# The square root of a piece's variance ahead of the first Silu, its normalisation ahead of the output weights, and the block decay kept by a maximum

## The chip, the cores and the metric

The kernel is written for one Trainium2 chip and runs on one of its cores. A core has five engines that work side by side: TensorE (PE), VectorE (DVE), ScalarE (ACT), GpSimd (POOL), and SyncE (SP), which here only issues DMAs. Each runs its own list of instructions in order and waits on semaphores. The metric is the time of one execution on the device, in microseconds; lower is better.

## The reference

`x` is (2, 1024, 512) in fp32. Two blocks follow each other, each with a layernorm ahead, a layernorm behind and a residual:

```
x = x + layernorm(attention(layernorm(x)))
x = x + layernorm(ffn(layernorm(x)))

attention(h):                        # 32 heads of 128
    q, k, v = silu(h @ qkv_w.T)      # per head
    # linear attention with a decay per head, in blocks; kv is the state
    scores = (q k^T) * diag_decay
    out    = scores v + (q * q_decay) kv
    kv     = kv * block_decay + (k * k_decay)^T v
    out    = norm_w * out * rsqrt(mean(out^2) + eps)
    return (sigmoid(h @ gate_w.T) * out) @ out_w.T
ffn(h):                              # 512 -> 1792 -> 512, integer weights with scales
    return (silu(h @ gate.T) * (h @ up.T)) @ down.T
```

The layernorm needs a mean and a variance of each token, and the square root of the variance plus 1e-5.

## The kernel before

**Tiling.** The tokens are cut into 16 tiles of 128, four segments of 512, two batches of 1024. The heads go in 16 pairs. One *step* `w` is a head pair of one batch; there are 32 steps (0 to 31), the 16 pairs for batch 0 and then the 16 for batch 1. Step 0 is written out apart. In step `w` the kernel projects K, Q, V and the gate G of that step, and finishes the attention and the output projection of the step before (`a = w - 1`). A projection is not a plain product: a 2x2 block scheme with seven products (numbered 1 to 7) and sums of their results (`keep_s1` on ACT, `keep_s2`, `keep_s3`, `finish_22`, `finish_12`, `finish_21` on DVE) takes the place of eight. Each fp32 operand is split in a high and a low part, so that each product is three matmuls for each of two row blocks.

**Order.** Every engine has a function `window(w, ...)` that writes out by hand the order of its instructions within a step; there is no planner. The engines keep together by counting semaphores alone. Hardware loops (`Fori`) repeat it. SP's `window` gives the order of the DMAs: weights, the K blocks written to DRAM (`k_write`, behind two transposes `turn_k` on DVE, line 1510) and read back turned (`k_read`), and the same for V (`v_write`, `v_read`, `turn_v` on line 1518).

**Pieces.** The input of batch 1 must be layernormed, transposed and put through the scheme's sums before step 16 needs it. That is spread over steps 1 to 8 as eight *pieces* of 2 x 128 tokens, the argument `part`. For a piece DVE takes statistics at the end of the step before (`statistics_of_piece`, the variance plus epsilon on line 1627, behind the two V transposes), ACT takes the root (`piece_root`, line 1012, both columns at once), DVE makes the reciprocal and the shift (`scales_of_piece`, lines 1633 and 1635), ACT normalises two tiles (`normalise_piece`, line 1018), PE transposes them (`turn_piece`, line 2189, four transposes ahead of product 7 of Q), ACT copies them out (`keep_piece`), DVE forms sums (`mix_piece`), ACT and POOL split and ACT stores them. From step 17 on, `finish` does the same for tiles of batch 0 ahead of the FFN; I call steps 18 to 25 tile steps. Steps 9 to 15 have no piece but a check of the FFN's integers on DVE (`look_at_block`, whose maximum is line 1570).

**ACT's tables.** Silu, Sigmoid and Sqrt each need another table of ACT. A load (`ACT_TABLE_LOAD`) stands in the trace ahead of an instruction whose table isn't the one that is loaded, and runs before that instruction's wait is over; none stands ahead of Copy, Square and Identity.

**The lines the prediction follows.** ACT, step `w`: `keep_s1(w, KK)` (Copy of K), Silu of K's block 11, `keep_s1(w, QQ)` (Copy of Q, line 910), then the root, `split_out_hi` (line 894, waits for the scaled output weights), `split_hi_s` (line 888), Silu of K's block 22 (line 926), `normalise_piece`, `square(a, 0, 0)` (line 940), `gated_hi`, `split_hi_a`, two Silus, `square(a, 0, 1)`. DVE: `gate(a, s, h)` (line 1555) waits for that Square, since it reads the same attention result; behind `gate(a, 0, 1)` come `turn_k(w, 1, 0)`, `turn_k(w, 1, 1)`, `update_state`, `keep_s3(w, QQ)` (line 1473), `turn_k(w, 0, 0)`, which waits until the K blocks are written (`k_out`), and `finish_22(w, QQ)` (line 1481). PE waits for `keep_s3` ahead of product 3 and for `finish_22` ahead of product 4:

```
                if i == 3:
                    pe.wait_ge(s3_done, n)
                if i == 4:
                    pe.wait_ge(c22_done, n)
```

`keep_b` (line 1534) saves the two block decays of a step out of `table`, 128 x 2 values, so that the table can be loaded anew while `update_state` of that step still needs them. It runs in each of the 32 steps.

Of the kernel before, what the change touches and what calls it, by code (L numbers as in the profile page):

```python
# [25 lines left out]
TAB_D, TAB_Q, TAB_K, TAB_B = 0, 2 * P, 4 * P, 4 * P + 2  # L26
# [50 lines left out]
def products_until(w, kind, i):  # L77

    if isinstance(w, int) and w == 0:
        return FIRST_ORDER.index((kind, i)) + 1  # L80
    return PRODUCTS * w - FEWER + ORDER.index((kind, i)) + 1
# [7 lines left out]
def sums_until(w, kind):  # L89

    return 4 * w + kind - 1
# [34 lines left out]
def sandwich_kernel(nc, x, w_attn, w_out, norm_w, tables, w_ints, ffn_scales, down_s, out):  # L126
    ctx = ExitStack()
    with ctx:
        def sem(name):
            return ctx.enter_context(nc.semaphore(name))  # L130

        def sb(name, shape, dt=F32, scope=ctx):
            return scope.enter_context(nc.sbuf_tensor(name, shape, dt))
# [24 lines left out]
        b_prev = sb("b_prev", [P, 2])  # L158
# [35 lines left out]
        table_in, b_kept = sem("table_in"), sem("b_kept")  # L194
# [70 lines left out]
        table = sb("table", [P, TAB], scope=two)  # L265
# [563 lines left out]
        def _(act):  # L829
# [83 lines left out]
            def activate(w, kind, out_block):  # L913

                n = sums_until(w, kind)
                dst = projected(kind, out_block)
                if out_block == OUT11:
                    act.wait_ge(proj_done, products_until(w, kind, 2))
                    src = blocks_view(kind, chain(kind, 0)[:, :])
                else:  # L920
                    act.wait_ge({OUT22: c22_done, OUT12: c12_done, OUT21: c21_done}[out_block], n)
                    src = dst
                if kind == GG:
                    act.activation(dst, src, ACT.Sigmoid).then_inc(gate_done, 1)
                else:
                    act.activation(dst, src, ACT.Silu).then_inc(silu_done, 1)  # L926
# [50 lines left out]
            def tile_root(i):  # L977

                act.wait_ge(tile_step, 5 * i + 3)
                act.activation(tile_stdev[:, 0:1], tile_var[:, 0:1], ACT.Sqrt).then_inc(tile_sd_ready, 1)  # L980
# [28 lines left out]
            def piece_root(j):  # L1009

                act.wait_ge(piece_step, 7 * j + 5)
                act.activation(tile_stdev[:, :], tile_var[:, :], ACT.Sqrt).then_inc(piece_sd_ready, 1)

            def normalise_piece(j):

                act.wait_ge(piece_step, 7 * j + 7)
                for s in range(HALVES):
                    act.activation(tiles[:, s], tiles[:, s], ACT.Identity, bias=tile_shift[:, s:s + 1],  # L1018
                                   scale=tile_rstd[:, s:s + 1]).then_inc(piece_normed, 1)
# [37 lines left out]
            def window(w, next_weights=True, checks=None, first_done=False, finish=None, begin=None,  # L1057
                       part=None, next_part=None, into_ffn=False):
# [6 lines left out]
                    square_root(norm_a[1])  # L1065
                if finish is not None:
                    tile_root(finish)
                activate(w, KK, OUT11)
                keep_s1(w, QQ)
                if part is not None:  # L1070
                    piece_root(part)
                split_out_hi(a)
                if finish is not None:
                    normalise_tile(finish)
                split_hi_s(w, VV)
                activate(w, KK, OUT22)
                if part is not None:
                    normalise_piece(part)
                square(a, 0, 0)
                gated_hi(a, 0, 0)  # L1080
                split_hi_a(w, VV)
# [299 lines left out]
        def _(dve):  # L1381
# [74 lines left out]
            def scale_out_weights(a):  # L1456
                dve.wait_ge(ow_in, 16 * (a + 1))
                dve.wait_ge(norm_in, 16 * (a + 1))
                for h in range(2):
                    dve.tensor_scalar(ow[:, h], ow[:, h], nw[:, h:h + 1], None,  # L1460
                                      ALU.mult).then_inc(ow_scaled, 1)
# [8 lines left out]
            def keep_s3(w, kind):  # L1470

                dve.wait_ge(proj_done, products_until(w, kind, 5))
                dve.tensor_tensor(projected(kind, OUT22), blocks_view(kind, chain(kind, 1)[:, :]),
                                  projected(kind, OUT12), ALU.add).then_inc(s3_done, 1)
# [56 lines left out]

            def keep_b(n):

                dve.tensor_copy(b_prev[:, :], table[:, TAB_B:TAB_B + 2]).then_inc(b_kept, 1)

            def update_state(a, s, h):
                dve.wait_ge(contrib_done, att_until(a, s, h))
# [92 lines left out]
            def scales_of_piece(j):  # L1630

                dve.wait_ge(piece_sd_ready, j + 1)
                dve.reciprocal(tile_rstd[:, :], tile_stdev[:, :]).then_inc(piece_step, 1)
                dve.wait_ge(piece_step, 7 * j + 6)
                dve.scalar_tensor_tensor(tile_shift[:, :], tile_meanvar[:, :, 0], -1.0, tile_rstd[:, :],
                                         ALU.mult, ALU.mult).then_inc(piece_step, 1)
# [11 lines left out]
            def window(w, first=False, checks=None, rms_of=None, ends_first=False, finish=None, begin=None,  # L1648
                       part=None, next_part=False, v_second=v_tok):
# [11 lines left out]
                if finish is not None:  # L1661
                    scales_of(finish)
                keep_s3(w, KK)
                scale_out_weights(a)
                finish_22(w, KK)
                finish_12(w, KK)
                if part is not None:
                    scales_of_piece(part)
                gate(a, 0, 0)
                finish_21(w, KK)  # L1670
                keep_s2(w, QQ)
# [768 lines left out]
```

## Time and profile before

| | us |
|---|---|
| median of 3 runs | 2396.22 |
| lowest and highest | 2396.11, 2396.77 |
| the profiled execution: first to last instruction (its span) | 2391.0 |
| busy: PE, POOL, DVE, ACT | 2350.5, 1679.5, 1379.5, 1207.6 |
| granted clock of PE, mean | 0.997 of full speed |

For the profiled execution the page gives the span alone; the time of an execution also holds what lies ahead of its first and behind its last instruction, so the span stands 5.2 us below the median of the runs. Busy times of the engines overlap. The ends of matmuls are modelled: an engine row of PE may run over the start of the next one, and the idle time in front of a PE row is then shown too short. The starts are measured.

### The profile page before, as it was taken

To read this page: it belongs to the slowest core of one execution; us is meant where nothing else is said; L and a number is where in the kernel's file an instruction comes from. 1 tells how busy PE (TensorE), PEld (TensorE's weight loads), DVE (VectorE), ACT (ScalarE), POOL (GpSimd) and SP (SyncE) were. 2 spreads that over 40 slices of the span, in tenths; PEclk is the share of its full clock that TensorE was granted. 3 is DMA by queue.
4 is the path that set the end of the run, shared out by engine and by line. 5 is a ranking of instruction groups with operands and counts; after the bars stand their busy time and mean duration, and the time that the engine had idled before them with its cause. 6 is when DMAs were issued, how large, how long until landed. Compare 5 with 4: busy or idle time off the path is not lost.

```text
span 2391.0 us, 38298 instructions
## 1 busy us (share of the span) xinstructions
PE 2350.5 (98%) x12276; PEld 2002.1 (84%) x12276; DVE 1379.5 (58%) x2475; ACT 1207.6 (51%) x1748; POOL 1679.5 (70%) x1322
## 2 busy tenths in 40 slices
PE   7999999999999999999999999999999999999997
PEld 6788888888888888878888888888888888888886
DVE  5555555555666666656555555555555555555655
ACT  6555555555444444435554555444444444466563
POOL 4667777777777777766777777777777776574675
PEclk9999999999999999999999999999999999999999
DMA  4334444444444444564443343444333333511212
GB/s 136 127 127 143 134 126 126 141 143 143 143 131 130 137 145 135 160 203 146 141 137 131 121 132 129 140 141 128 114 106 111 113 119 116 211 62 71 80 62 98
DMA packets 165954, 307.16 MB, mean 128 GB/s; under 512 B 22384, under 2 KB 102256, under 8 KB 163184
## 3 DMA queue, kind: packets, MB, share of 16 engines
q1 hardware_dynamic: 138992, 269.93, 34.7%
q10 hardware_dynamic: 26880, 36.18, 4.6%
q8 instruction: 46, 0.75, 0.1%
q14 instruction: 36, 0.29, 0.0%
HBM read 219.02 MB, written 87.03 MB: 128 GB/s over the span
## 4 chain that ended last, share of the span: by engine, by line
PE 89%; ACT 3%; DMA 3%; issue 2%; DVE 2%; POOL 0%; SPq 0%; DVEq 0%; ACTq 0%; POOLq 0%
PE proj L2012 54%; PE yp L2012 18%; PE sc L2059 5%; PE sc L2082 4%; PE sc L2085 4%; PE sc L2072 4%; DMA k_blocks<-pd 2%; DVE pd L1510 1%; ACT piece L1018 0%; ACT k L926 0%; ACT L926 0%; ACT sq L940 0%; DMA y<-x 0%; DVE g L1555 0%; ACT w_even L888 0%
## 5 line engine op out<-in xcount | busy, mean ns | idle before, releaser
L2012 PE MATMUL proj<-xb,w_odd 128*128 128x512 f32 x2694 | 704.9, 399 | 7.3 <-DVE q L1481 2.7
L2012 PE MATMUL proj<-xb,w_even 128*128 128x512 f32 x2694 | 678.4, 395 | 8.0 <-DVE xb L1425 3.3
L2012 PEld LDWEIGHTS proj<-xb,w_even 128*128 128x128 f32 x2694 | 496.9, 189 | 110.1 <-issue 5.9
L2012 PEld LDWEIGHTS proj<-xb,w_odd 128*128 128x128 f32 x2694 | 489.6, 189 | 106.2 <-DVE q L1481 6.9
L610 POOL TENSOR_TENSOR qd<-q,table 128x512 f32<-128x512 f32 x128 | 164.0, 1293 | 193.7 <-ACT q L926 193.7
L1555 DVE TENSOR_TENSOR g<-sc,g 128x512 f32<-128x512 f32 x128 | 88.4, 691 | 296.8 <-ACT sq L940 296.8
L601 POOL TENSOR_TENSOR ow_lo<-v_tok,ow_hi 128x1024 fp32r<-128x1024 f32 x32 | 76.7, 2397 | 224.0 <-ACT ow_hi L894 224.0
L1562 DVE TENSOR_TENSOR y<-yp,y 128x512 f32<-128x512 f32 x240 | 164.3, 685 | 120.5 <-PE yp L2012 119.2
L2012 PE MATMUL proj<-x_t,f_hi 128*128 128x512 f32 x896 | 212.6, 389 | 0.0
L2012 PE MATMUL yp<-ow_hi,g_hi 128*128 128x512 f32 x512 | 202.3, 395 | 0.3 <-issue 0.3
L595 POOL TENSOR_TENSOR w_odd<-ws,w_odd 128x1024 fp32r<-128x1024 f32 x63 | 151.3, 2401 | 69.5 <-ACT w_odd L888 69.5
L2012 PE MATMUL yp<-ow_hi,g_lo 128*128 128x512 f32 x512 | 199.5, 390 | 0.0
L2012 PE MATMUL yp<-ow_lo,g_hi 128*128 128x512 f32 x512 | 199.3, 389 | 0.0
L2012 PEld LDWEIGHTS proj<-x_t,f_hi 128*128 128x128 f32 x896 | 168.0, 188 | 34.9
L2082 PE MATMUL sc<-pd,v 128*128 128x128 f32 x1024 | 186.9, 274 | 0.0
L2085 PE MATMUL sc<-qd,state 128*128 128x128 f32 x896 | 173.2, 275 | 0.0
L626 POOL TENSOR_TENSOR g_lo<-g,g_hi 128x512 fp32r<-128x512 f32 x128 | 163.5, 1298 | 8.9 <-ACT g_hi L945 8.9
L2082 PEld LDWEIGHTS sc<-pd,v 128*128 128x128 f32 x1024 | 159.5, 191 | 10.0
L622 POOL TENSOR_TENSOR sumsq<-sumsq,sq 128x512 f32<-128x512 f32 x124 | 160.8, 1297 | 4.7
L731 POOL TENSOR_TENSOR h_lo<-hid,h_hi 128x512 fp32r<-128x512 f32 x56 | 73.3, 1310 | 112.1 <-ACT h_hi L1278 112.0
L933 ACT ACTIVATE kd<-k_tok,table 128x512 f32<-128x512 f32 x128 | 85.5, 716 | 131.4 <-DMA k_tok<-k_blocks 131.4
L595 POOL TENSOR_TENSOR w_even<-ws,w_even 128x1024 fp32r<-128x1024 f32 x63 | 151.9, 2411 | 0.0
(194 smaller groups left out, 4405.6 us busy)
## 6 DMA issues: line engine op xcount, KB each, us to landing
raw<-w_attn SPq DMA_DIRECT2D x128, 512.0 KB, 3.8
k_blocks<-pd SPq DMA_DIRECT2D x64, 512.0 KB, 3.6
k_tok<-k_blocks SPq DMA_DIRECT2D x256, 128.0 KB, 2.8
v_blocks<-vf SPq DMA_DIRECT2D x64, 512.0 KB, 2.7
v_tok<-v_blocks SPq DMA_DIRECT2D x248, 128.0 KB, 2.8
v_tok<-w_out SPq DMA_DIRECT2D x32, 512.0 KB, 4.5
fraw<-w_ints SPq DMA_DIRECT2D x13, 1024.0 KB, 4.8
piece<-w_ints ACTq DMA_DIRECT2D x21, 512.0 KB, 4.4
```

Source lines behind the costliest of these rows:

```text
L595: pool.tensor_tensor(w_lo[slot][:, S_1:S_4 + 1], ws[:, :, :, :], w_hi[slot][:, S_1:S_4 + 1].bitcast(F32), ALU.subtract).then_inc(wlo_s_don ...
L610: pool.tensor_tensor(qd[:, s, h].rearrange("p (c n) -> p c n", c=CH), q[:, h, half(s)].rearrange("p (c n) -> p c n", c=CH), decay.unsqueez ...
L622: pool.tensor_tensor(total, total, sq[:, h], ALU.add).then_inc(ss_done, 1)
L626: pool.tensor_tensor(g_lo[:, h], g[:, h, half(s)], g_hi[:, h].bitcast(F32), ALU.subtract).then_inc(glo_done, 1)
L933: act.activation(kd[:, s, h].rearrange("p c (i d) -> p i c d", i=QUADS), k_tok[:, :, h], ACT.Copy, scale=table[:, TAB_K + h:TAB_K + h + 1] ...
L1555: dve.tensor_tensor(at, sc[h][:, :], at, ALU.mult).then_inc(gated_done, 1)
L1562: dve.tensor_tensor(y[:, t], yp[t % 2][:, :], y[:, t], ALU.add).then_inc(yacc_done, 1)
L2012: last = pe.matmul(psum, s, m, start=start and n == 0, stop=n == len(terms) - 1, skip_group_check=more)
L2059: last = pe.matmul(sc[h][:, chunk(c)], k[:, h, tok], q[:, h, tok], start=True, stop=True)
L2072: last = pe.matmul(sc[h][:, chunk(c)], kd[:, s, h, c], v[:, s, c, h], start=True, stop=True)
L2082: last = pe.matmul(sc[h][:, chunk(c)], v[:, s, c, h], pd[:, s, h, c], start=True, stop=not inter)
L2085: last = pe.matmul(sc[h][:, chunk(c)], state[:, h, (c - 1) % CH], qd[:, s, h, chunk(c)], start=False, stop=True)
```

## The change

In steps 1 to 8 ACT takes the root of the piece's variance ahead of Silu of K's block 11, not behind the Copy of Q, and normalises the piece straight behind the Copy of Q, not behind Silu of K's block 22. DVE makes the piece's reciprocal and shift straight behind `keep_s3(w, KK)`, ahead of the scaling of the output weights, not behind `finish_12(w, KK)`. In all steps `keep_b` copies the two block decays by a maximum of them with themselves (`tensor_tensor` with `max`), where it was `tensor_copy`; the values are the same. No instruction is added or taken away in the code, no DMA and no semaphore changes.

```diff
--- before.py
+++ after.py
@@ -1065,17 +1065,17 @@
                     square_root(norm_a[1])
                 if finish is not None:
                     tile_root(finish)
+                if part is not None:
+                    piece_root(part)
                 activate(w, KK, OUT11)
                 keep_s1(w, QQ)
                 if part is not None:
-                    piece_root(part)
+                    normalise_piece(part)
                 split_out_hi(a)
                 if finish is not None:
                     normalise_tile(finish)
                 split_hi_s(w, VV)
                 activate(w, KK, OUT22)
-                if part is not None:
-                    normalise_piece(part)
                 square(a, 0, 0)
                 gated_hi(a, 0, 0)
                 split_hi_a(w, VV)
@@ -1531,7 +1531,8 @@
 
             def keep_b(n):
 
-                dve.tensor_copy(b_prev[:, :], table[:, TAB_B:TAB_B + 2]).then_inc(b_kept, 1)
+                kept = table[:, TAB_B:TAB_B + 2]
+                dve.tensor_tensor(b_prev[:, :], kept, kept, ALU.max).then_inc(b_kept, 1)
 
             def update_state(a, s, h):
                 dve.wait_ge(contrib_done, att_until(a, s, h))
@@ -1661,11 +1662,11 @@
                 if finish is not None:
                     scales_of(finish)
                 keep_s3(w, KK)
+                if part is not None:
+                    scales_of_piece(part)
                 scale_out_weights(a)
                 finish_22(w, KK)
                 finish_12(w, KK)
-                if part is not None:
-                    scales_of_piece(part)
                 gate(a, 0, 0)
                 finish_21(w, KK)
                 keep_s2(w, QQ)
```

## Rows read from the trace of the kernel before

Idle time ahead of an instruction stands in brackets, with what ended it. In the rows of stretches the columns are: from and to, length, then for PE, PEld, DVE, ACT and POOL the busy time with the number of instructions, PE's granted clock, DMA share and GB/s.

**Rows 1.** The page, part 1: busy time, share of the span, instructions.
```profile
PE 2350.5 (98%) x12276; PEld 2002.1 (84%) x12276; DVE 1379.5 (58%) x2475; ACT 1207.6 (51%) x1748; POOL 1679.5 (70%) x1322
```

**Rows 2.** Stretches: steps 1 to 8, step 8, step 9, one tile step.
```profile
74.13:589.90 515.77, 510.35 (x2716) 434.05 (x2715) 297.02 (x574) 274.19 (x409) 381.39 (x306) 1.00 0.42 132
525.25:589.90 64.65, 64.03 (x342) 54.41 (x341) 37.05 (x73) 34.22 (x52) 48.14 (x40) 1.00 0.42 131
589.90:652.56 62.66, 62.66 (x338) 53.97 (x337) 41.03 (x67) 29.20 (x43) 46.90 (x39) 1.00 0.43 140
1161.41:1224.54 63.13, 63.13 (x342) 54.31 (x341) 36.11 (x67) 31.63 (x48) 45.80 (x38) 1.00 0.40 133
```

**Rows 3.** Waits of PE, steps 1 to 8: us, times, longest.
```profile
PE proj L2012 <- DVE q L1481: 1.7, 5, 0.4
PE yp L2189 <- ACT piece L1018: 1.6, 6, 0.3
PE proj L2012 <- DVE q L1473: 0.7, 4, 0.2
PE proj L2012 <- DVE k L1473: 0.5, 2, 0.3
```

**Rows 4.** ACT in order of time, step 3: start, us.
```profile
202.86 0.60 ACT L910 ACTIVATE k<-proj 128x512 f32<-128x512 f32 x1 [0.96 <-PE proj L2012]
...
207.71 0.60 ACT L926 ACTIVATE k<-proj 128x512 f32<-128x512 f32 x1 [2.95 <-PE proj L2012]
211.33 0.60 ACT L910 ACTIVATE q<-proj 128x512 f32<-128x512 f32 x1 [3.03 <-PE proj L2012]
211.95 1.28 ACT L1012 ACT_TABLE_LOAD   x1
...
213.36 1.04 ACT L894 ACTIVATE ow_hi<-v_tok 128x1024 fp32r<-128x1024 f32 x1
...
215.36 1.28 ACT L926 ACT_TABLE_LOAD   x1
...
217.19 1.50 ACT L1018 ACTIVATE piece<-piece,tile_shift,tile_rstd 128x512 f32<-128x512 f32 x2
218.60 0.58 ACT L940 ACTIVATE sq<-sc 128x512 f32<-128x512 f32 x1
...
222.34 0.58 ACT L940 ACTIVATE sq<-sc 128x512 f32<-128x512 f32 x1
```

**Rows 5.** PE in order of time, step 3.
```profile
218.16 0.39 PE L2085 MATMUL sc<-qd,state 128*128 128x128 f32 x2
218.83 0.65 PE L2189 MATMUL yp<-ident,piece 128*128 128x128 f32 x4 [0.28 <-ACT piece L1018]
...
226.50 1.65 PE L2012 MATMUL proj<-xb,w_odd 128*128 128x512 f32 x6 [0.18 <-DVE q L1473]
...
229.86 1.66 PE L2012 MATMUL proj<-xb,w_odd 128*128 128x512 f32 x6 [0.34 <-DVE q L1481]
```

**Rows 6.** DVE in order of time, step 3.
```profile
206.05 0.47 DVE L1627 TENSOR_SCALAR tile_var<-tile_meanvar 128x2 f32<-128x2 f32 x1
...
211.06 0.88 DVE L1460 TENSOR_SCALAR v_tok<-v_tok,nw 128x512 f32<-128x512 f32 x2 [0.40 <-DMA nw<-norm_w]
...
223.56 1.29 DVE L1510 STREAM_TRANSPOSE pd<-k 128x512 f32<-128x512 f32 x2
...
228.52 0.71 DVE L1510 STREAM_TRANSPOSE pd<-k 128x512 f32<-128x512 f32 x1 [2.07 <-DMA k_blocks<-pd]
```

**Rows 7.** Single lines of DVE: ns min/median/max, first and last start in us.
```profile
L1534 DVE COPY b_prev<-table x32: 157/160/1536, 72.0 to 2036.1; 128x2 f32<-128x2 f32 x32
...
L1570 DVE TENSOR_TENSOR maxima<-maxima x21: 552/1021/1900, 609.3 to 1016.2; 128x1 f32<-128x1 f32 x21
...
L1635 DVE SCALAR_TENSOR_TENSOR tile_shift<-tile_meanvar,tile_rstd x8: 160/161/2292, 85.5 to 536.8; 128x2 f32<-128x2 f32 x8
```

**Rows 8.** DVE in order of time, step 8.
```profile
529.91 0.23 DVE L1627 TENSOR_SCALAR tile_var<-tile_meanvar 128x2 f32<-128x2 f32 x1
```

## The prediction

> **What bounds the kernel now.** I read the page first. TensorE (PE) is busy for 98% of the span [rows 1]. So an edit on ScalarE (ACT) or VectorE (DVE) can pay only where PE stands still, and the question is where, if anywhere, steps 1 to 8 hold it.
>
> The view of the stretches answers that [rows 2]. I cut it at the start of each step's first Copy of the K projection. Step 9 has no piece: 62.66 us, PE busy throughout. A tile step has the same four extra PE transposes as a piece step: 63.13 us, PE busy throughout. So 0.47 us is the fair price of four transposes. Steps 1 to 8 together take 515.77 us, where eight tile steps would take 505.04. The excess is 10.73 us, 1.34 us a step, and nothing else in the kernel runs at this discount. That is the most this change could give if it mended all of it. The idle time that the same row shows, 515.77 - 510.35 = 5.4 us, is smaller, because the modelled ends of matmuls run over part of each hole. I therefore use lengths, and the waits only for shares.
>
> The waits of PE in these eight steps name four releasers [rows 3]: the normalisation of the piece (1.6 us), DVE's line 1481 for Q (1.7), line 1473 for Q (0.7) and line 1473 for K (0.5). The first three are 4.0 of 4.5.
>
> Step 3 shows where they sit [rows 5]. The transposes of the piece start at 218.83, though PE's stream before them (pairs of 128-column matmuls from 218.16, a pair every 0.22) would be through at 218.39: a hole of 0.44. The row's own idle time is 0.28, so the modelled end hides 0.16. Product 3 of Q starts at 226.50 after 0.18 idle, so a hole of about 0.34; product 4 of Q at 229.86 after 0.34 idle, so about 0.50.
>
> ACT's order explains all three [rows 4]. After the Copy of Q at 211.33 it loads the square root's table (1.28), takes the root (0.13 to the next start), splits the output weights and the V sums, loads Silu's table again (1.28), runs a Silu, the two normalisations (1.50), and only then Square of head 0 (218.60) and of head 1 (222.34). DVE waits for that second Square: the K transposes start at 223.56, their write to DRAM has to land, the next transpose starts at 228.52 after a wait on that DMA, and behind it stands the finish of Q's block 22 that releases PE at 229.86 [rows 6]. Line 1473 for Q stands behind the same K transposes. So one lateness of ACT makes three holes. Meanwhile ACT idles 2.95 us ahead of its first Silu [rows 4].
>
> **The change, part by part.**
>
> *The root ahead of the first Silu.* It needs the variance, whose DVE instruction starts at 206.05 and takes 0.47, so 206.52 [rows 6]. The root's table is loaded before that: the load behind the Copy of K is through when the idle time begins, at 204.76. Then the root (to 206.7), the load of Silu's table (1.28 and a gap of some hundredths), and the first Silu starts near 208.1, not 207.71: 0.4 us later. The tile steps run just this order, and PE is busy throughout in them [rows 2]. Behind this Silu on ACT stands the Copy of Q at 211.33, with 3.03 us of idle before it. Cost: nothing. If the variance came after 209.2 (211.33 less 0.2 for the root, 1.3 and 0.6 for the Silu) the cover would be gone. That is 6.3 us into step 3, which starts at 202.86 [rows 4]. In step 8 the variance is done 4.9 us into the step (529.91 + 0.23 against 525.25), where step 3 has it after 3.7 [rows 2, 8]; 1.4 us are still left.
>
> *What leaves the stretch behind the Copy of Q.* Root's table and root 1.41 (from 211.95 to the next start, 213.36), Silu's table 1.28: about 2.7 us [rows 4]. The sequence has three table loads a step where it had four, and the one that is left over falls into ACT's idle time.
>
> *The normalisation ahead of the output weights.* It takes 1.41 us start to start (217.19 to 218.60), in the place where the load and the root took 1.41. The split of the output weights therefore still starts at about 213.4, GpSimd (POOL) and PE behind it see no change, and everything after Silu of block 22 comes 2.7 us sooner: Square of head 0 at 215.9, of head 1 at 219.6. PE has given attention of head 1 by 218.4, so that is not what holds it.
>
> *The scales on DVE.* Two small instructions, about 0.16 each [rows 7], move from behind the finishes of K to 210.66, where DVE is now free until 211.06 [rows 6]. They need the root, ready at 206.7. Behind them waits the scaling of the output weights, at 211.06 after 0.40 idle for a DMA: 0.36 with a gap fits in 0.40. Without that cover ACT would have the scaled weights 0.4 later (at 212.3), and it takes them at 213.4. Cost nothing.
>
> *The block decay by a maximum.* One DVE instruction of 128x2 in each of 32 steps, no DMA, no new wait. The copy takes 160 ns in the middle and 1536 at most [rows 7]. No maximum of this shape is in the trace. From below: a small DVE instruction on two SBUF inputs that nothing hinders, the shift at line 1635, is 160 at the least and 161 in the middle [rows 7]. From above: the 128x1 maximum of the width checks takes 552 to 1900, middle 1021 [rows 7]. So tiny an instruction can't be at work that long: something holds it. The copy is held too, up to 1.5 us, but in few steps, and what holds the one at this place in the step should hold the other. So I take the copy's time, a cost of 0; the upper end is the rival below. The Trainium skill (SBUF — State Buffer, section "Who interferes with whom") says that a DVE instruction with two SBUF inputs contends with a GpSimd instruction that reads SBUF, as does a copy in a two-port mode. By that rule both forms are exposed alike, the change of form buys nothing, and the rows agree as far as they go.
>
> *Where the stall goes.* Hole 1: the piece is normalised at about 213.3 and PE comes at 218.39: gone, 5 us of slack. Hole 2 and 3: K transposes at 220.9, the one behind the DMA at 225.8 with the same landing time, Q's block 22 ready for PE at 229.86 - 2.7 = 227.2. PE, now early by all three holes (0.44 + 0.34 + 0.50), wants it at 228.58. So 1.4 us of slack: gone as well. Line 1473 for Q has more. What is late next is that DMA: were it 1.4 us longer, hole 3 would come back.
>
> **Sum.** By shares, 10.73 x 4.0/4.5 = 9.5 us. Not mended directly is line 1473 for K, whose 0.5 us come from a late V transpose at the start of two steps. Since ACT and POOL get about 1 us further ahead of PE, one of these two (step 8) may close too; I add 0.2. Gain 9.7 us: the span 2391.0 becomes 2381.3. The runs' median 2396.22 lies 5.2 us above the profiled span, and I keep this distance: **2386.5 us**, 0.4% faster.
>
> **The rivals.**
>
> *A part of the holes stays.* The write of the K blocks, issued sooner beside a weight load, takes over 1.4 us longer in some steps, or DVE reaches line 1473 late for another reason. Then PE keeps hole 3, or 2 and 3. For it speaks that this DMA is in the path; against it that the landing now is followed by slack. Keeping hole 3 in all steps (1.7 of 4.5, of 10.73) costs 4.1: gain 5.6, 2390.6.
>
> *The releasers named are not the real ones.* PE's holes in 2 and 3 might be the DMA's alone, whatever ACT does, and the first hole moves to the next wait. Against it stand steps 9 and on, without root or normalisation and with no hole [rows 2]. Then at most the transposes' hole goes (1.6 of 4.5, of 10.73: gain 3.8, 2392.4), at least nothing (2396.2); both are within 0.2%.
>
> *Slower: the maximum is held by POOL everywhere.* If it waits for a whole POOL operation (the longest of the checks' maxima, 1.9 us) in each of 31 steps, the V transposes, the V read behind them and line 1473 for K are late in the next step. Step 8 shows the price: the variance, which stands behind these transposes, starts 4.66 us into the step against 3.19 in step 3, and these 1.47 gave a hole at K's product 3 of about 0.44 (its longest wait, 0.3, and the 0.16) [rows 3, 6, 8]. So a hold counts from about 1.03 us. At 1.9 in 31 steps: 31 x 0.87 = 27 lost, 9.7 gained, 2413. It decides from 1.03 + 9.7/31 = 1.34 us in every step. Against it: the copy takes 160 ns in the middle, so nothing holds it in most steps.
>
> *The table loads cost more than their rows.* The Trainium skill (ScalarE: Activation LUTs, section "What ACT_TABLE_LOAD costs") puts a drain of about 1.4 us on top of the load; here the next instruction starts 1.30 us after the load's start, so the trace doesn't show it. By the page ACT would gain still more, and the time would be the same, since PE is the limit.
>
> **How the numbers follow.** All three holes go (gain 8.4 to 10.9: from a step or two that keeps one, to all of the excess): 0.77. A part stays: 0.12. Not the real releasers: 0.07 (within 0.2%). Slower by the maximum: 0.04. The runs differ by 0.7 us and a measurement can tell 0.2%, 4.8 us, from no change. Likeliest 2386.5; its own range 2385.0 to 2388.0. The range of 8 in 10 reaches a little into the partial case: 2384.6 to 2389.8. Faster by over 0.2%: 0.77 + 0.12 = 0.89; within 0.2%: 0.07; slower 0.04.
>
> **What the profile after would show.** Steps 2 to 7 are 63.1 us long, where 515.77/8 is 64.5, and PE is busy in all of the stretch. ACT has the root at about 206.7 in step 3's place, three table loads a step, the normalisation straight behind the Copy of Q. PE waits neither for line 1018 nor for line 1481. The copy's successor takes 0.16 us in most steps and up to 1.5 in some. Wrong would be: steps that stay at 64; a wait of PE on the K write's chain at the old place; a DVE instruction of over 1 us at the decay in most steps, with longer steps from 9 on.

## The result and the profile after

The changed kernel takes 2383.6 us, median of 5 executions (2382.43 to 2384.59), against 2396.11 for the kernel before, also 5 (the three behind 2396.22 and two more; 2393.24 to 2396.77). The ratio is 0.9948, with a 95% interval of 0.9937 to 0.9958. The change gains 12.5 us, where 9.7 were forecast. The time lies 1.0 us below the foot of the range that I gave. In the experiments further down, one of the 11 executions of before_again took 11691 us at a granted clock of 0.19, and its ratio leaves that one out.

The profiled execution of the changed kernel took 2383.29 us for a span of 2381.4. The page, part 1, of the kernel after:

```profile
PE 2345.7 (98%) x12276; PEld 2002.7 (84%) x12276; DVE 1381.2 (58%) x2475; ACT 1196.6 (50%) x1740; POOL 1678.2 (70%) x1322
```

ACT has eight instructions fewer than in [rows 1], 1740 for 1748: one table load less in each piece step. DVE and POOL are as they were.

Stretches of the kernel after: steps 1 to 8, then step 3, step 5 and step 9 (columns as in [rows 2]).

```profile
73.23:579.10 505.87, 504.38 (x2715) 433.97 (x2715) 297.94 (x574) 263.42 (x402) 381.47 (x306) 1.00 0.42 135
199.03:261.96 62.93, 62.93 (x341) 54.27 (x340) 37.54 (x73) 32.83 (x50) 47.16 (x39) 1.00 0.43 137
325.17:389.56 64.39, 64.39 (x349) 55.51 (x348) 36.18 (x72) 32.81 (x50) 47.05 (x39) 1.00 0.39 126
579.10:641.76 62.66, 62.66 (x338) 53.95 (x337) 41.44 (x67) 29.29 (x43) 46.26 (x39) 1.00 0.42 136
```

The first row stands against 515.77 in [rows 2]: 9.90 us less. Step 3 is 62.93 long; before it was 64.48. Step 9, without a piece, has its old length to the hundredth (62.66). The one piece step that still stands out is step 5 with 64.39. The waits of PE in steps 1 to 8 show the same (us, times, longest):

```profile
PE proj L2013 <- DVE k L1467: 0.8, 1, 0.8
PE proj L2013 <- DVE k L1473: 0.6, 2, 0.3
```

Of [rows 3] only line 1473 for K is left. The normalisation and both waits of Q are gone, in all eight steps. Line 1467 for K is new, once (in step 6, behind the long step 5; see "What stays open").

ACT in step 3, whose first Copy starts at 199.03, 3.83 us sooner than in [rows 4]. To compare two rows, take each from its own step's start.

```profile
199.03 0.60 ACT L910 ACTIVATE k<-proj 128x512 f32<-128x512 f32 x1 [1.37 <-PE proj L2013]
199.65 1.28 ACT L1012 ACT_TABLE_LOAD   x1
202.32 0.20 ACT L1012 ACTIVATE tile_stdev<-tile_var 128x2 f32<-128x2 f32 x1 [1.39 <-DVE tile_var L1628]
202.54 1.28 ACT L926 ACT_TABLE_LOAD   x1
203.88 0.60 ACT L926 ACTIVATE k<-proj 128x512 f32<-128x512 f32 x1
207.51 0.60 ACT L910 ACTIVATE q<-proj 128x512 f32<-128x512 f32 x1 [3.03 <-PE proj L2013]
208.00 1.51 ACT L1018 ACTIVATE piece<-piece,tile_shift,tile_rstd 128x512 f32<-128x512 f32 x2
...
211.83 0.58 ACT L940 ACTIVATE sq<-sc 128x512 f32<-128x512 f32 x1
...
215.57 0.57 ACT L940 ACTIVATE sq<-sc 128x512 f32<-128x512 f32 x1
```

The root starts 3.29 us into the step and the first Silu at 4.85, which was 4.85 before too (207.71 - 202.86): the load and the root are covered. The Square of head 1 starts 16.54 us into the step, where it was 19.48: 2.94 sooner.

DVE in step 3:

```profile
206.95 0.16 DVE L1636 SCALAR_TENSOR_TENSOR tile_shift<-tile_meanvar,tile_rstd 128x2 f32<-128x2 f32 x1
...
216.78 1.29 DVE L1510 STREAM_TRANSPOSE pd<-k 128x512 f32<-128x512 f32 x2
...
223.01 0.71 DVE L1510 STREAM_TRANSPOSE pd<-k 128x512 f32<-128x512 f32 x1 [2.32 <-DMA k_blocks<-pd]
223.65 0.65 DVE L1481 TENSOR_TENSOR q<-proj,q 128x512 f32<-128x512 f32 x1
```

The product of PE that [rows 5] had wait for line 1481 starts at 224.62, with no idle time ahead of it.

The K transposes start 17.75 us into the step, 2.95 sooner than in [rows 6] (20.70). But the transpose behind the DMA starts at 23.98, against 25.66: only 1.68 sooner. So 1.27 us of the gain went between the two, and SP's queue shows where. First before, then after (start, duration of the issue):

```profile
223.48 0.33 SPq L378 DMA_DIRECT2D raw<-w_attn  x1
224.88 0.33 SPq L395 DMA_DIRECT2D k_blocks<-pd  x1
228.51 1.76 SPq L402 DMA_DIRECT2D k_tok<-k_blocks  x4
```

```profile
217.25 0.33 SPq L378 DMA_DIRECT2D raw<-w_attn  x1
218.11 0.33 SPq L395 DMA_DIRECT2D k_blocks<-pd  x1
223.00 1.75 SPq L402 DMA_DIRECT2D k_tok<-k_blocks  x4
```

The reads of line 402 wait until the K write of line 395 has landed. Before, the write was issued 1.40 us behind the weight load and 3.63 us later it had landed. After, it stands 0.86 behind the load and takes 4.89. The other steps are alike: in the eight piece steps the write is 1.40 to 1.54 behind and lands in 3.35 to 3.70 before, 0.77 to 0.90 behind and in 4.38 to 4.89 after. DVE has `finish_22(Q)` at 223.65 + 0.65 = 224.30 and PE comes at 224.62: 0.3 us of slack, where I had counted 1.4.

### The profile page after: what moved, and what is told of

Read it like the earlier page. It is cut to its first block, busy times and chain, and to the rows that moved or that the text cites. A ratio compares the mean times of both kernels' runs of the same rounds, so it can differ in the third digit from the quotient of the medians.

```text
span 2381.4 us, 38290 instructions
## 1 busy us (share of the span) xinstructions
PE 2345.7 (98%) x12276; PEld 2002.7 (84%) x12276; DVE 1381.2 (58%) x2475; ACT 1196.6 (50%) x1740; POOL 1678.2 (70%) x1322
## 4 chain that ended last, share of the span: by engine, by line
PE 79%; issue 1%; DMA 1%; DVE 1%; POOL 1%; ACT 1%; SPq 0%; DVEq 0%; ACTq 0%; POOLq 0%
PE proj L2013 48%; PE yp L2013 16%; PE sc L2083 4%; PE sc L2060 4%; PE sc L2086 3%; PE sc L2073 3%; DMA k_blocks<-pd 0%; DMA v_tok<-v_blocks 0%; DMA k_tok<-k_blocks 0%; DMA v_blocks<-vf 0%; POOL w_odd L588 0%; PE yp L2181 0%; PE sc L2121 0%; ACT sq L940 0%; DVE pd L1510 0%
## 5 line engine op out<-in xcount | busy, mean ns | idle before, releaser
L2083 PEld LDWEIGHTS sc<-pd,v 128*128 128x128 f32 x1024 | 160.0, 191 | 10.1
```

Source lines behind the costliest of these rows:

```text
L2083: last = pe.matmul(sc[h][:, chunk(c)], v[:, s, c, h], pd[:, s, h, c], start=True, stop=not inter)
```

## The experiments

Twelve runs were made, in three groups, each with executions of the kernel before on the same chip (medians 2397.55, 2398.07 and 2397.54 in the groups). I give the ratio to these. "Steps 1 to 8" is the length of that stretch in the one profiled execution. All theories are about these steps. The rest of the span is 1873.5 to 1880.3 us long in the fourteen traces, whatever the order in the piece steps (before 1875.2, before_again 1878.2, after 1875.5, order_only 1877.9).

**The kernel before, once more** (before_again). No edit.

> The kernel before, unchanged, to see how its executions spread and how span and time stand to each other. Theory: the time is the span plus about 1.9 us, as in the five executions of the changed kernel (1.9 to 2.1), and the profiled execution of before (span 2391.0) was a short one; most executions then have a span of about 2394.2, and the 3 us lie in places that one trace doesn't show. Rival: before really has 5.2 us around its span; then its spans are near 2391.0 in every execution. Time 2396.1 by both.

2396.42 us, ratio 0.9998 (0.9988 to 1.0007). Its stretches: steps 1 to 8, then step 5; and PE's waits in steps 1 to 8.

```profile
73.73:591.95 518.22, 510.88 (x2718) 434.57 (x2717) 303.15 (x574) 274.02 (x410) 381.27 (x306) 1.00 0.41 131
...
331.81:398.34 66.53, 65.88 (x355) 56.04 (x353) 38.91 (x72) 34.12 (x52) 47.84 (x39) 1.00 0.39 123
```

```profile
PE proj L2012 <- DVE q L1481: 2.5, 8, 0.5
PE yp L2189 <- ACT piece L1018: 1.9, 7, 0.3
PE proj L2012 <- DVE k L1467: 1.3, 1, 1.3
PE proj L2012 <- DVE q L1473: 0.8, 5, 0.2
```

The same program is 2.45 us longer in these steps than in the trace that I had. Step 5 alone makes 2.1 of it (66.53 against 64.40): at its end DVE was late, since a V read landed late, and ACT's next Copy of K came late behind it; PE then waited 1.34 us for line 1467, 5.14 us into step 6. The other steps differ from the trace before by less than 0.2 us each. The profiled execution took 2398.45 us for a span of 2396.4, and in every execution whose span is listed, of every kernel, the time is 1.86 to 2.15 us above the span. The 21 executions of the kernel before in this group have spans of 2391.9 to 2399.7 with a median of 2395.5. So the execution behind [rows 1 to 8], with 2391.0, was a short one.

**The order alone, and the maximum alone** (order_only, max_only).

```diff
# order_only
+                if part is not None:
+                    piece_root(part)
                 activate(w, KK, OUT11)
                 keep_s1(w, QQ)
                 if part is not None:
-                    piece_root(part)
+                    normalise_piece(part)
                 split_out_hi(a)
...
                 activate(w, KK, OUT22)
-                if part is not None:
-                    normalise_piece(part)
...
                 keep_s3(w, KK)
+                if part is not None:
+                    scales_of_piece(part)
                 scale_out_weights(a)
                 finish_22(w, KK)
                 finish_12(w, KK)
-                if part is not None:
-                    scales_of_piece(part)
```

```diff
# max_only
-                dve.tensor_copy(b_prev[:, :], table[:, TAB_B:TAB_B + 2]).then_inc(b_kept, 1)
+                kept = table[:, TAB_B:TAB_B + 2]
+                dve.tensor_tensor(b_prev[:, :], kept, kept, ALU.max).then_inc(b_kept, 1)
```

> The moves on ScalarE and VectorE alone, the block decay still a copy. Theory: all of the gain is the moves', 2383.6 us, within 0.7. Rival: the maximum makes the 2.8 us by which the prediction fell short, and this kernel takes 2386.4.

> The maximum alone, in the old order. Theory: no change, 2396.1 us. Rival 1: the maximum is worth 2.8 us, 2393.3. Rival 2: the maximum costs, by up to 1.3 us beside GpSimd in 8 steps, and the moves gained more than they showed: 2397 to 2398.

The order alone: 2383.72 us, 0.9943 (0.993 to 0.9957), steps 1 to 8 504.24. PE waits once in them, 0.3 us for line 1473 of K in step 1, and steps 2 to 8 are 62.93 to 63.21 long.

```profile
74.25:578.49 504.24, 503.95 (x2718) 434.26 (x2717) 299.45 (x574) 263.07 (x401) 381.43 (x306) 1.00 0.43 135
```

The maximum alone: 2396.0 us, 0.9996 (0.9987 to 1.0005), steps 1 to 8 517.73. The whole gain is the order's.

The decay's instruction by itself: the copy in before_again, then the maximum in max_only (ns min/median/max).

```profile
L1534 DVE COPY b_prev<-table x32: 157/164/3118, 72.1 to 2041.3; 128x2 f32<-128x2 f32 x32
```

```profile
L1535 DVE TENSOR_TENSOR b_prev<-table x32: 139/156/3117, 72.6 to 2039.2; 128x2 f32<-128x2 f32 x32
```

Both forms are held, and up to the same 3.12 us.

**The root early, the normalisation where it was** (root_only): order_only without the move of `normalise_piece`.

> Root ahead of the first Silu and scales early, normalisation at its old place behind Silu of block 22, block decay a copy. Theory: what counts is the 2.7 us of table loads and root that leave ScalarE's stretch ahead of the two Squares; the normalisation stands ahead of them either way, so 2383.6 us like the moves together. Rival: the place of the normalisation counts by itself (the piece ready 5 us ahead of TensorE's transposes rather than 2.4): 2386 to 2388.

2383.76 us, 0.9944 (0.9931 to 0.9958), steps 1 to 8 504.16. The move of the normalisation adds nothing that can be measured to the moves of the root and the scales. It even costs slack. SP in step 3 of root_only, which starts at 200.37:

```profile
218.19 0.33 SPq L378 DMA_DIRECT2D raw<-w_attn  x1
219.57 0.33 SPq L395 DMA_DIRECT2D k_blocks<-pd  x1
223.38 1.75 SPq L402 DMA_DIRECT2D k_tok<-k_blocks  x4
```

Here the write stands 1.38 us behind the weight load and lands in 3.81, and `finish_22(Q)` is through 1.3 us ahead of PE (224.67 against 225.95), where the kernel after has 0.3. The rows say what the normalisation has to do with it. The load is issued when POOL's line 588 has ended (218.02 here, 218.14 in order_only, with the load at 218.30). That line waits for ACT here. In order_only the output weights' split comes later behind the normalisation, POOL starts on its sums 1.3 us later in the step and runs through without a gap, and the load goes out 0.4 us later in the step (18.21 against 17.82), while the write goes out 0.1 us sooner.

**The scales left behind the finishes of K** (scales_late): order_only without DVE's part.

```diff
# scales_late: order_only, but with
                 keep_s3(w, KK)
-                if part is not None:
-                    scales_of_piece(part)
                 scale_out_weights(a)
                 finish_22(w, KK)
                 finish_12(w, KK)
+                if part is not None:
+                    scales_of_piece(part)
```

> ScalarE as in the change, but VectorE makes the piece's scales at the old place, behind the finishes of K (to 213.84 in step 3 of before); block decay a copy. The normalisation then holds ScalarE for 1.9 us behind the Copy of Q. Theory: what counts is when the two Squares come; here they come 0.9 us earlier than before where the change gives 2.9. Hole 1 goes, hole 2 all but goes, of hole 3 about 0.4 us a step stays: steps of 63.5 us, 2387 us, against 2383.7 with the scales early. Rival: the scales' place does not matter, 2383.7.

2397.26 us, 0.9999 (0.9991 to 1.0008), steps 1 to 8 517.71. No gain at all, where I had expected 2387. Its waits of PE in steps 1 to 8, then PE and SP in step 3, which starts at 204.06:

```profile
PE proj L2012 <- DVE q L1481: 10.1, 8, 1.5
```

```profile
231.21 1.65 PE L2012 MATMUL proj<-xb,w_odd 128*128 128x512 f32 x6 [1.40 <-DVE q L1481]
```

```profile
224.23 0.33 SPq L378 DMA_DIRECT2D raw<-w_attn  x1
225.09 0.33 SPq L395 DMA_DIRECT2D k_blocks<-pd  x1
229.86 1.75 SPq L402 DMA_DIRECT2D k_tok<-k_blocks  x4
```

The waits for the normalisation and, but for 0.2 us in step 1, for line 1473 of Q are mended, as in the kernel after. Yet product 4 of Q starts 27.15 us into the step, and in the kernel before it started at 27.00 (229.86 - 202.86, [rows 4, 5]). ACT is 1 us sooner here (DVE has the K transposes at 223.77, 19.71 into the step, against 20.70), but the write is again 0.86 behind the weight load and lands in 4.77 us instead of 3.63, which takes that 1 us back. So the start of product 4 is set by the chain through the K write alone; in all eight steps PE waits for line 1481 there, 0.92 to 1.54 us. Holes 1 and 2 ahead of it only shorten hole 3: closing them gives nothing as long as that chain ends last.

**The pieces' root left out** (no_table): the old order, with the piece's square root replaced by a Copy, so that no table is loaded for it. The pieces are then scaled wrongly.

```diff
-                act.activation(tile_stdev[:, :], tile_var[:, :], ACT.Sqrt).then_inc(piece_sd_ready, 1)
+                act.activation(tile_stdev[:, :], tile_var[:, :], ACT.Copy).then_inc(piece_sd_ready, 1)
```

> The old order and the old copy, but the piece's root is replaced by a Copy: the square root is left out for the pieces, and with it two table loads a step. Theory: the two loads (2.6 us ahead of the Squares) are the cost, not the order in itself; 2383.7 us and steps of 63.1. Rival: the order matters by more than its loads (the normalisation ahead of the transposes): 2386 to 2388, with a wait of TensorE for the normalisation left.

2387.28 us, 0.996 (0.9947 to 0.9973), steps 1 to 8 507.68. With the old order kept and only the two table loads out of ACT's stretch, three quarters of the gain are there (9.6 us by the ratio, where the kernel after has 12.5). The time is not the 2383.7 of my theory but lies where the rival had it. The rival's sign, a wait of PE for the normalisation, is absent all the same: steps 2, 3, 4, 7 and 8 have the lengths of the kernel after to 0.01 us, with the root, the scales and the normalisation all at their old places. What is missing in the trace against the kernel after, 1.8 us, is in step 1 (64.07 against 62.75, with 0.3 us of wait left for line 1481) and in steps 5 and 6. What makes the rest of the 2.9 us between the two gains no trace shows. ACT gains less here than the loads give, since DVE's shift, at its old place but sooner, is held for about 2 us in every step and the normalisation waits for it (1.05 us in step 3):

```profile
L1635 DVE SCALAR_TENSOR_TENSOR tile_shift<-tile_meanvar,tile_rstd x8: 1966/2032/2299, 85.7 to 529.4; 128x2 f32<-128x2 f32 x8
```

So the K transposes start 19.14 us into step 3, 1.56 sooner than before, but the write keeps its 1.39 behind the load and lands in 3.54, and hole 3 is closed. It is the loads that held ACT, not the place of the root as such.

**The normalisation early, the root late** (norm_early_root_late): one move more in the old order.

```diff
                 if part is not None:
                     piece_root(part)
+                    normalise_piece(part)
...
                 activate(w, KK, OUT22)
-                if part is not None:
-                    normalise_piece(part)
```

> Root at its old place behind the Copy of Q, the normalisation straight behind it, VectorE in the old order, four table loads a step, block decay a copy. TensorE finds the piece ready. Theory: the wait for the normalisation goes, but the Squares come 0.4 us later than before, so holes 2 and 3 grow by what hole 1 gives back and 0.4 more: steps of 64.9 us, 2399.5 us. Rival: the three holes are separate, and the first one's share is gained: 2392.4.

2404.91 us, 1.0032 (1.0021 to 1.0043), steps 1 to 8 523.77: 7.7 us slower than the kernel before by the ratio, where I had expected 2399.5. In its step 3 (start 204.81) ACT waits for the scales, and Square of head 1 comes 0.72 us later in the step than before, not 0.4:

```profile
216.01 1.52 ACT L1018 ACTIVATE piece<-piece,tile_shift,tile_rstd 128x512 f32<-128x512 f32 x2 [0.61 <-DVE tile_shift L1634]
```

PE then waits most for line 1472 of that kernel (1473 of the kernel before), 6.4 us in eight waits. So the early normalisation does harm unless the root and the scales are early too, and with them it gives nothing (root_only). The root's move alone, with the scales and the normalisation at their old places, wasn't run. No_table, which has both at their old places and no loads, gives every step but 1, 5 and 6 its full gain; this suggests that the root's move alone would do most of it, but doesn't show it.

**The decay's instruction behind the V transposes** (decay_late): the kernel after, with `keep_b(w)` moved behind `turn_v(w, 0, 0)` and `turn_v(w, 0, 1)` in every step that begins no tile, steps 1 to 8 among them.

> The changed kernel, with the maximum behind the two V transposes of head 0 and 1 rather than ahead of them. In the changed kernel it is held by up to 1.4 us in steps 1 to 8, beside GpSimd. Theory: this hold has cover (the V transposes have 1 us to spare in most steps), so within 0.2% of it, at most 0.5 us faster: 2383.2. Rival: the hold still costs some tenths in each of the eight steps and is behind the hole at step 5: 2381 to 2382.

2385.45 us, 0.9952 (0.9939 to 0.9965), steps 1 to 8 505.38. No gain over the kernel after. My rival of 2381 to 2382 isn't borne out; that the instruction is held at that place costs nothing that can be measured.

**The K write ahead of the weight load** in SP's queue, in the kernel of scales_late, the kernel before and the kernel after (scales_late_kfirst, before_kfirst, after_kfirst), with the kernel after once more beside them (after_again).

```diff
-                if next_weights:
-                    weights(w + 1, KK, ...)
-                k_write(w, 1)
+                k_write(w, 1)
+                if next_weights:
+                    weights(w + 1, KK, ...)
                 k_read(w, 1)
```

> As the kernel with the late scales, which gained nothing though two of the three holes had gone, but SyncE issues the write of the second segment's K blocks ahead of the next step's K weights, not behind them. In the kernel with the late scales the write came 0.86 us behind that weight load and took 4.7 us to land, where in before it came 1.4 behind it and took 3.6. Theory: the write shares the DMA engines with the weight load, and that took back what the earlier Squares gave; without the load ahead it lands in about 3 us and hole 3 (1.3 to 1.6 us a step) goes: 2384 to 2387 us. Rival: the landing has nothing to do with the load, hole 3 stays: 2396 to 2397.

> The kernel before with only that exchange on SyncE. Theory: hole 3 (0.2 to 0.7 us a step) goes, since it is set by the landing, and holes 1 and 2 stay; gain 8 x 0.5 = 4 us, 2392 to 2393, and a smaller spread of the executions. Rival: no change, 2396.4.

> The changed kernel with that exchange on SyncE. TensorE finds Q's block 22 ready 0.3 us ahead in the changed kernel; with the write landing in 3 us and not 4.9 it would be 2 us ahead. Theory: nothing to gain any more in most steps, 2383.6, at most 1 us less. Rival: the later K weights delay the sums of GpSimd and so later steps: 2384 to 2386.

> The changed kernel once more, on the chip on which the kernel before has its time of 2396 to 2398, for a second trace. Theory: 2383.6, span 1.9 to 2.1 below the time, steps 1 to 8 together 504 to 506 us against 517 to 518 in the traces of the old order; the late V read at step 5 is in some traces and not in others. Rival: the gain of 12.5 was the chip's, and here it is 9.7.

| kernel | us | ratio | steps 1 to 8 |
|---|---|---|---|
| scales_late_kfirst | 2384.04 | 0.9944 (0.9931 to 0.9958) | 506.54 |
| before_kfirst | 2389.95 | 0.9971 (0.996 to 0.9982) | 511.47 |
| after_kfirst | 2383.91 | 0.9938 (0.9924 to 0.9951) | 504.19 |
| after_again | 2383.1 | 0.9937 (0.9923 to 0.9951) | 506.37 |

SP of scales_late_kfirst in step 3 (start 200.23):

```profile
221.37 0.33 SPq L395 DMA_DIRECT2D k_blocks<-pd  x1
221.99 0.33 SPq L378 DMA_DIRECT2D raw<-w_attn  x1
224.29 1.76 SPq L402 DMA_DIRECT2D k_tok<-k_blocks  x4
```

The write is issued 21.14 us into the step, no sooner than in scales_late (21.03), and lands in 2.92 us instead of 4.77. The 10.1 us of waits for line 1481 are gone (what is left of PE's waits in the eight steps is 0.9), and the kernel gains what the kernel after gains. So what took scales_late's gain was the write's landing behind the weight load.

PE's waits of before_kfirst in steps 1 to 8:

```profile
PE yp L2189 <- ACT piece L1018: 2.2, 8, 0.3
PE proj L2012 <- DVE k L1467: 1.3, 1, 1.3
PE proj L2012 <- DVE q L1473: 1.1, 7, 0.2
```

Here hole 3 is gone and holes 1 and 2 are left. Steps 2 to 8 are 63.84 to 64.12 long, each 0.85 to 0.93 more than the same step of order_only, where the prediction had read 0.44 + 0.34 = 0.78 for the two. This exchange alone gets 0.9971, about half of the change's gain. On the kernel after it adds nothing that can be measured: the 0.3 us of slack is enough there.

## Why the prediction was right in its mechanism and short in its size

**The bound and its place**, that PE stands still only in steps 1 to 8 and at three holes in each: right. All three are gone in all eight steps, and in step 3 the root is through 3.49 us into the step (202.32 + 0.20 - 199.03), where the working had 3.84 (206.7 - 202.86), since the variance is ready sooner too. So the rivals by which the releasers aren't the real ones, or a part of the holes stays, are out for this kernel.

**The root ahead of the first Silu**, covered by ACT's idle time: right (first Silu 4.85 us into the step before and after; the 0.4 us by which the working had it later didn't come). **What leaves the stretch**, 2.7 us of loads and root: right, the Square of head 1 comes 2.94 sooner; no_table shows that it is the loads. The 0.24 beyond 2.7 are gaps that went with them: where no load stands between, ACT's next instruction starts some 0.1 us before the end of the one ahead (the normalisation at 208.00, the Copy of Q until 208.11).

**The scales on DVE, "Cost nothing"**: true of their price, but with the normalisation early they carry the result: scales_late gains nothing. I had called that move free where it was needed. With the normalisation at its old place the late scales don't stop the gain (no_table), so the need is one that the early normalisation makes.

**The block decay by a maximum, a cost of 0**: right, by max_only, though the argument's top, "up to 1.5 us, but in few steps", was low: the copy is held in most of steps 1 to 8, and for 3.12 us in one of before_again. The rival that went by this hold is out: both forms are held alike.

**"With the same landing time"**: wrong. The write lands in 4.9 us instead of 3.6, since DVE comes 2.9 us sooner and the weight load ahead of it in the queue only 2.4 (18.22 into the step for 20.62). Of "1.4 us of slack" 0.3 was left. The sentence that the gain would fail "were the DMA 1.4 longer" was the right one: it got 1.27 longer in step 3. The kernel after escapes by 0.3; scales_late, where ACT gains only 1 us, doesn't. In root_only the landing is nearly the old one (3.81) and the slack 1.3, as counted: what broke the premise is the early normalisation, by way of POOL and the weight load.

**The sum is the step that failed: "By shares, 10.73 x 4.0/4.5 = 9.5", with its 0.2 a "gain 9.7".** It gave 9.7 where 12.5 were measured. The mechanism was right, the term was mis-sized, and three things are in it.

First its form. Holes on one path don't add up as shares. The K write's chain lets product 4 start 27.00 us into the step, and PE without holes is there at 25.59 (224.62 - 199.03): this difference of 1.41 is nearly all of the 1.55 by which step 3 became shorter. Closing the two holes ahead of it would have given nothing, as scales_late shows, and the rival "keeping hole 3 costs 4.1" should have read: costs nearly all. Since all three close, all of the excess of 10.73 goes and not 9.7: 1.0 us more.

Second the length without holes. I took eight tile steps, 505.04. In order_only and root_only the eight piece steps take 504.24 and 504.16: 0.8 us less. So the 10.73 that the prediction called the most the change could give was no ceiling. Like for like, with neither trace holding the late V read, the order is worth 515.77 - 504.2 = 11.6 us.

Third the trace. The measured gains are 12.5 us for the kernel after, with an interval of 10 to 15 (0.42 to 0.63% of 2396), and 13.4 to 15.1 by the ratios of order_only, root_only and after_again. The intervals of the first three hold 11.6, only that of after_again (11.8 to 18.5) doesn't, so the 1 to 3.5 us above 11.6 may be noise in part. What isn't noise is most likely in executions of the kernel before that are longer than the one profiled: steps 1 to 8 are 517.2 on average in the three traces of the old order (before, before_again, max_only), and even these have a mean span, 2393.8, below the median of 2395.5. Which waits make the longest executions long, no trace shows.

**"The runs' median 2396.22 lies 5.2 above the profiled span, and I keep this distance"** amounts to the median less the gain, and in that form it holds. But the distance isn't one of the program. 2.0 us of it are there in every execution; the other 3.2 say that the profiled execution was that much shorter than the median one. The agreement of my span, 2381.3, with the 2381.4 of the profiled execution after is therefore an accident: a short execution less a gain that was too small met an ordinary one, among five spans of 2380.5 to 2382.7.

**What stays open.** A late V read makes step 5 longer in eight traces, of both orders (66.53 in before_again, 66.58 in max_only, 67.11 in norm_early_root_late, 64.74 in no_table, 64.39 in the kernel after, 64.95 in after_again, 65.53 in decay_late, 64.1 in scales_late_kfirst). In the other six (before, order_only, root_only, scales_late, before_kfirst, after_kfirst) step 5 has the length of its neighbours. In the kernel after DVE waited 3.43 us for the read, ACT's Copy of K that ends step 5 came late behind that, and PE waited 0.81 for line 1467 in step 6; steps 5 and 6 together are 1.67 us longer than in order_only:

```profile
385.91 0.71 DVE L1518 STREAM_TRANSPOSE v<-v_tok 128x512 f32<-128x512 f32 x1 [3.43 <-DMA v_tok<-v_blocks]
```

```profile
394.75 1.65 PE L2013 MATMUL proj<-xb,w_even 128*128 128x512 f32 x6 [0.81 <-DVE k L1467]
```

Why it lands late in some executions no run tells. My 0.2 for one of the waits of line 1473 for K did not come: both are there after the change, 0.6 us in all.

## What to carry to other kernels

When a chain and a few holes ahead of it end at the same wait, don't add the holes up: work out when the chain's end and the engine's own arrival come, and price each edit by the later of the two. And when an edit is a bundle, run each move alone and each left out: here one of three moves gave nothing and used up the slack of the others. A transfer on such a chain must be priced again when its issue moves, since its landing can hang, as it did here, on what stands just ahead of it in the queue. And set the profiled execution's own time, or its span with the constant distance, against the median first: if it was a short one, a span that comes out as forecast proves nothing.

## What the runs showed of the hardware

A 512 KB write, issued behind a 512 KB load from the same queue, landed in 3.6 us where it stood 1.40 us behind, in 4.8 and 4.9 us at 0.86 behind, and in 2.9 us ahead of the load (step 3 of before, scales_late, after, scales_late_kfirst). Over the eight piece steps these are 3.35 to 3.70, 4.36 to 4.88, 4.38 to 4.89 and 2.88 to 2.93 us. All are times from the write's issue to the issue of the read that waits for it.

A DVE instruction on 128x2 values that takes 0.14 to 0.16 us when nothing holds it stood for up to 3.12 us beside GpSimd, as a copy and as a maximum alike. DVE and POOL of before_again in step 5:

```profile
390.09 3.12 DVE L1534 COPY b_prev<-table 128x2 f32<-128x2 f32 x1
```

```profile
389.26 1.85 POOL L588 TENSOR_TENSOR w_even<-raw,w_even 128x768 fp32r<-128x768 f32 x1
391.06 0.74 POOL L573 TENSOR_TENSOR ws<-raw 128x256 f32<-128x256 f32 x1
391.76 0.73 POOL L575 TENSOR_TENSOR ws<-raw 128x256 f32<-128x256 f32 x1
392.46 0.73 POOL L578 TENSOR_TENSOR ws<-ws,raw 128x256 f32<-128x256 f32 x1
393.26 0.74 POOL L581 TENSOR_TENSOR ws<-raw,ws 128x256 f32<-128x256 f32 x1
```

The copy ends at 393.21, between the end of line 578's sum (393.19) and the start of line 581's (393.26). The ends of the three POOL instructions before, each overlapped by the start of the next in these rows, didn't release it. The Trainium skill (SBUF — State Buffer, section "Who interferes with whom") lets a DVE instruction with two SBUF inputs contend with a GpSimd instruction that reads SBUF, and says of DVE's two-port modes, which a copy can enter, that whichever instruction issues first has the shared ports for all of its length and the other is blocked. The trace agrees that the copy and the maximum are held beside POOL (3.12 us each); whether the copy ran in such a mode no trace shows. A hold for the length of one POOL instruction is in step 3 of no_table: the shift starts at 211.94 and stands until 214.04, and the POOL sum that started at 211.62 ends at 214.01. But in before_again the copy outlasts three ends of POOL instructions. That it waits for a gap in POOL's stream is what these rows suggest; no run tried it apart.
